# Expert turns inside the up blocks, slots listed six experts ahead, and a centred output projection in a layer on one core

## The reference

```python
x = L0_attn_x                                                   # (4, 2048, 512) float32
x = x + _layernorm(_L0_attn_ref(_layernorm(x), w_qkv, w_out, sorf_signs, sorf_scales))
x = x + _layernorm(_L0_ffn_ref(_layernorm(x), gate_w, bias, W1, W3, W2, sw1, sw3, sw2))
# attention: q_phi, k_phi = 128 exponential features a head (16 heads);
#   out = (q_phi @ (k_phi^T v)) / max(q_phi @ sum(k_phi), 1e-6);  return out @ w_out.T
# ffn: 32 experts, 4 a token, at most 512 tokens an expert (capacity); width 512 -> 256 -> 512
#   h = silu(xe @ W1) * (xe @ W3);  ye = h @ W2;  out = sum of the 4 weighted rows + shared expert(sw1, sw3, sw2)
```

## Time and profile before

| what | value |
|---|---|
| median of 3 runs | 2131.86 us (2129.33 to 2133.62) |
| the profiled execution's own time | 2130.38 us |
| its span, first to last instruction | 2128.0 us |
| PE busy | 1829.2 us (86%) |
| DVE busy | 1280.8 us (60%) |
| ACT busy | 938.7 us (44%) |
| POOL busy | 770.3 us (36%) |
| mean granted clock of PE | 0.947 |

### The profile page before, as it was taken

How to read it: one execution, slowest core, us unless ns; L and a number is a source line. 1 busy time by engine, 2 the same in 40 slices (tenths; PEclk the granted TensorE clock), 3 DMA queues, 4 the chain that set the end, 5 groups by cost and what they waited for, 6 DMA issues and landing times.

```text
span 2128.0 us, 31538 instructions
## 1 busy us (share of the span) xinstructions
PE 1829.2 (86%) x11952; PEld 894.7 (42%) x11952; DVE 1280.8 (60%) x2358; ACT 938.7 (44%) x1243; POOL 770.3 (36%) x718
## 2 busy tenths in 40 slices
PE   8999999999969998787888886446888888887785
PEld 5444444444448883232333332313444444443332
DVE  6877676767610000378788888753555555555886
ACT  3444444444346665465656654312333333322343
POOL 0000000000000000126777777874777777751110
PEclk9999999999979999999999998777999999999997
DMA  6544444445368884678778756343898999868983
GB/s 218 187 144 169 149 165 157 157 170 184 120 176 212 211 211 113 165 205 235 202 218 237 204 187 200 119 164 82 179 213 220 233 240 231 199 136 234 328 300 137
DMA packets 188695, 404.98 MB, mean 190 GB/s; under 512 B 33668, under 2 KB 71940, under 8 KB 171920
## 3 DMA queue, kind: packets, MB, share of 16 engines
q1 hardware_dynamic: 83040, 222.38, 36.8%
q10 hardware_dynamic: 68640, 124.26, 16.2%
q0 software_dynamic: 36864, 56.32, 13.4%
HBM read 237.03 MB, written 177.08 MB: 195 GB/s over the span
## 4 chain that ended last, share of the span: by engine, by line
DVE 23%; PE 18%; DMA 6%; issue 6%; POOL 4%; ACT 4%; SPq 1%; POOLq 0%; DVEq 0%; ACTq 0%
PE s_gates L1474 6%; PE s_ups L1474 6%; DVE s_xT L1607 4%; DVE s_y L1622 3%; DMA s_spread<-share_dram 3%; POOL slot_dram L1252 3%; PE s_y L895 2%; DVE s_heads L1092 2%; DVE s_h L1597 1%; DVE s_stats L1646 1%; DVE s_x L1665 1%; DVE s_at_hl L1096 1%; ACT s_parts L1533 1%; ACT s_gate L1527 1%; PE s_logits L864 1%
## 5 line engine op out<-in xcount | busy, mean ns | idle before, releaser
L258 PE MATMUL s_proj<-s_xT,keep_wqkv 128*128 128x512 f16 x1536 | 344.2, 379 | 0.0
L1252 POOL DMA_INDIRECT slot_dram<-keep_filled,keep_slots x256 | 277.7, 1085 | 104.6 <-issue 74.0
L1417 POOL DMA_INDIRECT acc_dram<-s_y,s_slot x128 | 200.4, 1566 | 113.3 <-DVE s_y L1622 68.5
L895 PE MATMUL s_y<-keep_wo,s_at_hl 128*128 128x512 f16 x768 | 195.5, 409 | 40.1 <-ACT s_z L984 40.1
L258 PEld LDWEIGHTS s_proj<-s_xT,keep_wqkv 128*128 128x128 f16 x1536 | 149.1, 98 | 180.2 <-issue 12.6
L1527 ACT ACTIVATE s_gate<-s_gates 128x512 f32<-128x512 f32 x96 | 57.1, 597 | 292.7 <-PE s_ups L1474 247.3
L338 POOL TENSOR_SCALAR s_rstd<-s_mv 128x4 f32<-128x4 f32 x16 | 16.0, 1000 | 462.6 <-DVE s_mv L353 462.6
L1597 DVE SCALAR_TENSOR_TENSOR s_h<-s_gate,s_ups 128x512 f32<-128x512 f32 x96 | 65.8, 686 | 187.8 <-ACT s_gate L1527 187.8
L235 PE MATMUL s_proj<-keep_wqkv,s_xT 128*128 128x512 f16 x768 | 172.9, 382 | 4.9 <-DVE keep_wqkv L404 4.9
L963 ACT ACTIVATE s_phi<-s_logits 128x1024 f32<-128x1024 f32 x128 | 131.5, 1027 | 92.0 <-PE s_logits L864 91.3
L674 ACT ACTIVATE s_phi<-s_logits 128x1024 f32<-128x1024 f32 x128 | 131.1, 1024 | 86.2 <-PE s_logits L695 86.2
(11 more groups left out here) (164 smaller groups left out, 3241.5 us busy)
## 6 DMA issues: line engine op xcount, KB each, us to landing
s_x<-x_in SPq DMA_DIRECT2D x32, 1024.0 KB, 10.4
qk_dram<-s_hl ACTq DMA_DIRECT2D x32, 1024.0 KB, 7.1
keep_ahead<-qk_dram SPq DMA_DIRECT2D x48, 512.0 KB
acc_dram<-s_zero SPq DMA_DIRECT2D x17, 1024.0 KB, 8.9
v_dram<-s_v ACTq DMA_DIRECT2D x16, 1056.0 KB, 4.0
s_v<-v_dram SPq DMA_DIRECT2D x16, 1056.0 KB, 11.1
s_spread<-share_dram SPq DMA_DIRECT2D x64, 256.0 KB
x_dram<-s_x ACTq DMA_DIRECT2D x16, 1024.0 KB, 7.8
```

What stands on the lines that cost most here:

```text
L258: mm = nc.tensor.matmul(out[:, 512 * b:512 * b + 512], left, right, start=(c == 0 and i == 0), stop=(c == EC - 1 and i == 2))
L895: mm = nc.tensor.matmul(y[m % 2][:], at_hl[n % 2][:, s, c, a * P:(a + 1) * P], keep["wo"][:, w, c, :], start=(c == 0 and i == 0), stop=(c ...
L1252: nc.gpsimd.indirect_dma_start(out=io["slot"], out_offset=bass.IndirectOffsetOnAxis(ap=slots[n % 2][:, a * K + j:a * K + j + 1], axis=0), ...
L1417: nc.gpsimd.indirect_dma_start(out=io["acc"], out_offset=bass.IndirectOffsetOnAxis(ap=slot[e % RING][:, a, 0:1], axis=0), in_=y[e % 2][:, ...
```

## The change

Attention. Stage 1 takes the mean over the output columns away from `w_out` before it is split (`centre_wo` on DVE, beside group 1), so that y has mean zero and its norm needs no shift. `make_z` on ACT goes; `add` on DVE forms y * rstd + x straight from the bank, which now frees the bank. `make_shift` makes only the shift of x1. With one stage of the pipeline gone, all lags from ADD on fall by one, those of `choose`, `weigh`, `count`, `fill` and `send` among them, while `read_total`, `make_share`, `divide` and `make_at_low` keep theirs: the work once in four steps falls on other steps.

Experts. PE turns the next expert's blocks inside `up`, one ahead of each block of 8 matmuls, and no longer between the parts of `down`; ACT and DVE are put in an order that follows this. DVE copies the first two parts of y ahead of `low(1)`. POOL does `add(e)` ahead of a gather, which is now that of expert e + 6; slot lists have ten buffers, `rows` still three, and a gather still waits until the expert three before it is turned.

```diff
+            def centre_wo():
+                dve.wait_ge(w_out_loaded, 16)
+                nc.vector.tensor_reduce(wo_mean[:], w_out[:], AX.X, ALU.add).then_inc(wo_summed, 1)
+                dve.wait_ge(wo_summed, 1)
+                nc.vector.scalar_tensor_tensor(out=w_out[:], in0=wo_mean[:].unsqueeze(2).broadcast_to([P, EC, E]),
+                                               scalar=-1.0 / E, in1=w_out[:], op0=ALU.mult,
+                                               op1=ALU.add).then_inc(wo_centred, 1)
...
+                if n == 1 and j == 3:
+                    centre_wo()
...
-        PROJECT, MEASURE, SCALE, ADD, SPLIT, TURN, COPY, GATE = 8, 9, 10, 11, 12, 13, 14, 14
-        SCORE, CHOOSE, PLACE, WEIGH, FILL, SEND = 18, 18, 19, 19, 21, 21
+        PROJECT, MEASURE, ADD, SPLIT, TURN, COPY, GATE = 8, 9, 10, 11, 12, 13, 13
+        SCORE, CHOOSE, PLACE, WEIGH, FILL, SEND = 17, 17, 18, 18, 20, 20
...
                 if m >= 2:
-                    pe.wait_ge(z_ready, m - 1)
+                    pe.wait_ge(x1_ready, m - 1)
...
-                nc.scalar.activation(z[k][:], y[k][:], ACT.Identity, bias=shift[k][:, 0:1],
-                                     scale=rstd[k][:, 0:1]).then_inc(z_ready, 1)
...
-                dve.wait_ge(z_ready, m + 1)
+                dve.wait_ge(rstd_ready, m + 1)
...
-                nc.vector.tensor_tensor(x[n % XS][:, a, :], x[n % XS][:, a, :], z[m % 2][:], ALU.add).then_inc(x1_ready, 1)
+                nc.vector.scalar_tensor_tensor(out=x[n % XS][:, a, :], in0=y[m % 2][:], scalar=rstd[m % 2][:, 0:1],
+                                               in1=x[n % XS][:, a, :], op0=ALU.mult, op1=ALU.add).then_inc(x1_ready, 1)
...
-        RING, AHEAD = 6, 3
+        RING, ROWS, AHEAD = 10, 3, 6
...
             for e in range(NE):
+                add(e)
                 if e + AHEAD < NE:
                     gather(e + AHEAD)
-                add(e)
...
-                    for bank, w in ((gates[i], w_gate), (ups[i], w_up)):
+                    for k, (bank, w) in enumerate(((gates[i], w_gate), (ups[i], w_up))):
+                        if ahead is not None:
+                            turn(ahead, 2 * i + k)
...
                 for a in range(A):
-                    if p - NS + 2 < NE:
-                        turn(p - NS + 2, a)
                     down(p, a)
...
+            for e in range(-1, NE):
+                more = e + 2 < NE
+                if more:
+                    make_xT_low(e + 2, 0)
+                    make_xT_low(e + 2, 1)
+                hidden(NS + e + 1, 0)
+                if more:
+                    make_xT_low(e + 2, 2)
+                low(NS + e + 1, 0)
+                if more:
+                    make_xT_low(e + 2, 3)
+                hidden(NS + e + 1, 1)
+                if e >= 0:
+                    down(e, 0)
+                    down(e, 1)
+                low(NS + e + 1, 1)
+                if e >= 0:
+                    down(e, 2)
+                    down(e, 3)
```

More of the change, by code:

```diff
@@ L1297, in expert_and_combine_programs @@
         slot = [t.sb(f"slot{r}", [P, A, 2], U32) for r in range(RING)]
-        rows = [t.sb(f"rows{r}", [P, A, E]) for r in range(AHEAD)]
+        rows = [t.sb(f"rows{r}", [P, A, E]) for r in range(ROWS)]
         xT = t.pair("xT", [P, 2, EC, G], F16)
@@ L1313, in expert_and_combine_programs @@
             [t.sem(f"{n}{k}") for k in range(2)] for n in ("w_loaded", "w2_loaded", "added", "y_stored"))
-        gathered = [t.sem(f"gathered{r}") for r in range(AHEAD)]
+        gathered = [t.sem(f"gathered{r}") for r in range(ROWS)]
         slot_loaded = [t.sem(f"slot_loaded{r}") for r in range(RING)]
@@ L1458, in up @@
                 e = p - NS
+                ahead = e + 1 if 0 <= e < NE - 1 else None
                 if 0 <= e < NE:
@@ L1502, in pe_program @@
             up(NS)
-            for a in range(A):
-                turn(1, a)
             for p in range(NS, PASSES):
@@ L1667, in dve_program @@
             wait_routed(dve)
-            for r in range(AHEAD):
+            for r in range(ROWS):
                 for a in range(A):
@@ L1681, in dve_program @@
                 make_xT_low(0, a)
-            for i in range(IC):
-                hidden(NS, i)
-                low(NS, i)
-            for a in range(A):
-                make_xT_low(1, a)
-            for e in range(NE):
-                for i in range(IC):
-                    hidden(NS + e + 1, i)
-                    low(NS + e + 1, i)
-                down(e)
+            for e in range(-1, NE):
+                more = e + 2 < NE
+                if more:
+                    make_xT_low(e + 2, 0)
+                    make_xT_low(e + 2, 1)
+                hidden(NS + e + 1, 0)
+                if more:
+                    make_xT_low(e + 2, 2)
+                low(NS + e + 1, 0)
+                if more:
+                    make_xT_low(e + 2, 3)
[7 more added lines that the diff above has]
+                    down(e, 3)
             for q, n in enumerate(ORDER):
```

113 lines of the change are left out of this document (50 added, 63 removed).

## The result

The changed kernel takes 2146.77 us (median of 7 runs, 2140.41 to 2152.78), the kernel before on the same chip 2131.10 (2128.55 to 2136.44). The ratio is 1.0076, 95% interval 1.0057 to 1.0096: 16 us slower, where 2075 us were forecast. The profiled execution has a span of 2144.9 us and took 2146.77.

What follows compares the result with a forecast made beforehand. It took waits to bound attention, where no engine is full, and PE, 89% busy, plus waits the experts. 2130.4 + 1 (centring) - 26.5 (attention) - 31 (experts) = 2073.9, with 1.5 for the median 2075 us; range 2052 to 2106.

Steps and rivals of the forecast that it cites:

- the cost of the new places of the group work: Attention: DVE's work spread over other steps makes a group 30.3 us instead of 32.0, 19 us won in all.
- The wait for `dens`, 1.9 us: Attention: DVE's wait for `dens`, 21.1 / 11 from the earlier trace, counted inside the new 9.2 us step.
- One step less in the pipeline, -6.5 and -1: Attention: all sends come one step of 6.5 us sooner, and 1 more for a long DVE step before the first send.
- Centred weights, +1 of 0 to 6.9: Stage 1: two DVE operations of 4.6 to 6.9 us, once, beside PE; cost taken as 1 us, bounds 0 to 6.9.
- z removed: Attention: ACT loses 64 operations; DVE's `add` reading the bank may cost 0 to 0.1 us a step.
- Expert loop, -31: Experts: shorter expert periods and an earlier start win 31 us, bounds -11 to -48.
- The middle term: Expert loop: the middle 19 experts take 13.65 us each instead of 14.25, a gain of 0.6 each, 11.4 in all.
- POOL's additions keep the loop: Rival, expert loop: landings don't get shorter, POOL holds 14.1 us, only the ends gain 11; 2095 us, chance 0.20.
- slower case: Rival, expert loop: SP's loads meet every expert's additions, landings come late, 42 us lost; 2148 us, chance 0.04.
- The gathers six ahead: Expert loop: they cost and give nothing, since `rows` keeps three buffers and PE waits for rows only at the first expert.
- Attention keeps 32.0: Rival, attention: the 9.2 us step with `dens` replaces the 9.7 one, only 7.5 is won; 2094 us, chance 0.14.
- signs of being wrong: Landing waits of 1.3 us or more or `down` copy awaiting `added`; `dens` waits from 3 us, 32 us groups; PE idle before 555.

Runs made afterwards that it cites:

- e9: e8 with ACT making the high part of the quotient (`make_at_high`) one step later, behind both exponentials; 2088.1 us, ratio 0.9814 to the kernel before.
- e8: e5 with the centring cut in two, sums beside group 1 and subtraction beside group 2; 2112.4 us, ratio 0.9919 to the kernel before.
- e3: Changed kernel with ACT's `make_score` waiting only for that group's choice, not for the slot lists of the group before; 2120.2 us, ratio 0.9941 to the kernel before.
- e4: Changed kernel with DVE taking the shares, and so waiting for `dens`, behind `fill` instead of ahead of it; 2118.6 us, ratio 0.9937 to the kernel before.
- e11: Changed kernel with POOL's old order: gathers three experts ahead, each ahead of the additions, six slot lists; 2158.4 us, ratio 1.0152 to the kernel before.
- e5: Changed kernel with the edits of e3 and e4 together; 2116.8 us, ratio 0.9928 to the kernel before.
- e12: Changed kernel with only the high part of the quotient made later on ACT; 2145.0 us, ratio 1.0069 to the kernel before.
- e15: Changed kernel with ACT's three 1 MB stores a group issued one step later, as in the kernel before; 2143.1 us, ratio 1.0051 to the kernel before.
- e6: Changed kernel with the thirteen 1 MB loads moved behind the expert loop; 2141.0 us, which contains the wait for the late loads.

## Why the prediction was wrong, step by step

*The step that failed: the cost of the new places of the group work.* It was taken as 19 us won; the ten periods alone lost 19.0. DVE's work in each step was sized well, but even the repaired kernel's period is above its sum: e9, with almost no wait for `dens` left, needs 29.8 us where the same steps add up to 28.4. What failed is that the sum counted what DVE does in a step and how long PE can wait for DVE, and not who else waits for what was moved. `fill` went behind the wait for `dens`; `make_score`, which waits for it, stands at the head of ACT's step, ahead of the exponential. ACT's wait for `keep_slots` was in the trace of before, 32.3 us in the stretch of the earlier trace rows, and in no row that I took. The lower bound "nothing at all" came from DVE's and POOL's times alone and left out a loss. Measured: +1.9 us a group from group 1 on, where -1.7 was taken.

*The wait for `dens`, 1.9 us.* It was taken from the earlier trace rows for another place. It was 3.8 there, although DVE asked for it about as long after `read_total` as before (4.4 us in the rows shown, 4.7 in the group of the earlier trace rows): the trip itself got longer. The stores that moved with the lags were not counted.

*One step less in the pipeline, -6.5 and -1.* The step itself seems to be there: in e8, whose attention starts as early as that of before, the first send comes at 954.25 us (962.49 in the earlier trace rows), though e8 has the repairs of e3 and e4 too. In the changed kernel the same late steps ate it: counted from attention's start it came 2.5 us sooner, and group 1 already later.

*Centred weights, +1 of 0 to 6.9.* The operations were sized well (4.57 us, the low end of 4.6 to 6.9), the hiding was not: 5.8 us of delay, within the bounds. The loss of clock behind PE's wait was not counted. The text named the work queued behind them, the next group's normalising, and then took DVE's 28% of free time as if it lay at that place.

*z removed.* Right: the add from the bank takes 0.74 us instead of 0.68, and PE's wait for the bank is small, 4.5 us. In part that is because PE is held elsewhere: in e3 it waits 25.5 us there, 8.3 at the longest.

*Expert loop, -31, measured -8.* PE's work of 12.2 us is right, and the last five cycles and the start came as taken (-5 and -7.5 for -5 and -6). The middle term failed: 13.65 was taken, 14.80 measured, against 14.15 before. Taken together, the 26 cycles ahead of the last five lost 4 us where the sum won 20. The rival "POOL's additions keep the loop" had the mechanism, but with no change as its worst end for the middle. With PE ahead of POOL, SP's loads, which follow PE, met the landings; the prediction had this as its slower case, with attention's gain against it.

*The gathers six ahead "cost and give nothing".* Wrong, together with "POOL's order of `add` before `gather` changes nothing": without both the kernel loses another 16 us (e11), and no run takes back only one. The turns inside `up` let PE run nearly one expert further ahead of POOL (SP's loads, which follow PE, come that much sooner), and then the place of a gather in POOL's order decides whether rows are there; they have three buffers in either kernel.

*The rivals.* "Attention keeps 32.0" named the right step, the wait for `dens` in the 9.2 us step, but its price ended at no gain. The slower rival's 2148 meets the kernel's 2147 by luck: it put the loss in the loop and kept attention's gain. Three of the signs of being wrong came: a first `down` copy that waits for `added` (the row at 1669.54), waits for `dens` above 3 us, and PE idle before 555 us (the row at 134.39).

## What to carry to other kernels

When work moves to another place in an engine's order, list for each semaphore that it raises who waits for it, where that waiter stands in *its* engine's order, and what stands behind the waiter; a sum of one engine's work by steps holds only when no other engine stands in front of a late result with urgent work behind it. Such waits hide one another (e3, e4 and e5 gave nearly the same, e12 alone nothing, and e9 on top of them 22 us by the ratios), so after each repair the list of waits is read again. Transfers that move with the work, and loads whose time follows an engine that was made faster, belong in the sum like instructions.

## What the runs showed of the hardware

Small transfers pay for large ones beside them: the trip of `den` (four writes of 8 KB, a load of 32 KB) takes 4.9 to 5.5 us in most groups of the kernel before, and 7.0 to 9.0 in most groups of the changed one, where a store of 1 MB is issued 2.5 us after its start. In e15, with that store away and another one ahead, the other half of the trip is the longer one. An expert's fourth addition lands 7.5 us after its issue in the mean of the loop's middle before, 8.3 in the changed kernel with the same bytes, and 6.7 with the loads of 1 MB out of the loop (e6). A reduction over 128x2048 on DVE takes 2.28 us, as long as an operation that writes all 2048 columns (2.29).
